# A network block on one core: front, first memory step and read-out in another order

## The reference

```
x = x + L0_conv(_ln_c(x))     # a memory: 16 steps over t, each one gradient step on a two-layer MLP per batch
t = t + L0_ffn(_ln_t(t))      # router, 8 experts, two chosen per token: gelu(xe @ W1 + b1) @ W2 + b2
x = x + L1_conv(_ln_c(x))     # small convolutions, applied over and over on channel groups
t = t + L1_ffn(_ln_t(t))      # a gated recurrence over 256 positions

def step(carry, x_t):                       # of L0_conv
    k = _l2norm(x_t @ Wk); v = x_t @ Wv
    lr, forget, eta = (means over c of sigmoid(x_t @ w_...))
    g = grad_fn(params, k, v)               # grad of mean((mlp(params, k) - v)**2)
    new_mom = eta * mom - lr * g;  new_params = params * (1 - forget) + new_mom
final = mean over b of paramsT;  return mlp(final, q)      # q = _l2norm(x @ Wq), the read-out
xe = xn * ln_g + ln_b                       # of L0_ffn, for each expert
```

## Time and profile before

| what | us |
|---|---|
| median of 3 runs (589.94 to 596.36) | 595.57 |
| the profiled execution, its own time | 592.88 |
| its span, first to last instruction | 591.1 |
| TensorE busy in the span | 537.3 |
| VectorE busy | 285.9 |
| ScalarE busy | 217.6 |
| GpSimd busy | 104.3 |

### The profile page before, as it was taken

How to read it: one execution, slowest core, us unless ns; L and a number is a source line. 1 busy time by engine, 2 the same in 40 slices (tenths; PEclk the granted TensorE clock), 3 DMA queues, 4 the chain that set the end, 5 groups by cost and what they waited for, 6 DMA issues and landing times.

```text
span 591.1 us, 10757 instructions
## 1 busy us (share of the span) xinstructions
PE 537.3 (91%) x3798; PEld 310.1 (52%) x3798; DVE 285.9 (48%) x1320; ACT 217.6 (37%) x1084; POOL 104.3 (18%) x103
## 2 busy tenths in 40 slices
PE   6799999999987999898799999999999999999996
PEld 4598888888744433377354444444444444444443
DVE  2636666666644744701734444444444444444443
ACT  1425555555423634010133333333333333333332
POOL 3227777777810000000000000000000000000000
PEclk9759999999988999999889999999999999999998
DMA  7400000000000000000000000000000000000000
GB/s 216 202 2 0 2 2 1 2 2 1 2 0 1 0 1 2 0 1 0 1 2 1 1 2 1 2 1 2 2 1 2 1 2 1 1 2 0 2 2 19
DMA packets 2871, 7.12 MB, mean 12 GB/s; under 512 B 1404, under 2 KB 1985, under 8 KB 2625
## 3 DMA queue, kind: packets, MB, share of 16 engines
q1 hardware_dynamic: 2818, 6.44, 3.1%
HBM read 6.18 MB, written 0.26 MB: 11 GB/s over the span
## 4 chain that ended last, share of the span: by engine, by line
PE 52%; DVE 24%; ACT 16%; issue 7%; POOL 1%; DVEq 0%; POOLq 0%
PE bk L652 14%; DVE bk L1143 8%; ACT gi L813 8%; DVE mem L1146 7%; ACT bk L817 6%; PE bk L538 4%; PE bk L609 4%; PE bk L556 2%; PE bk L463 2%; PE bk L422 2%; PE bk L444 2%; PE bk L432 2%; PE bk L362 1%; PE bk L355 1%; PE bk L394 1%
## 5 line engine op out<-in xcount | busy, mean ns | idle before, releaser
L668 PE MATMUL bk<-idle 128*64 128x512 bf16 x720 | 201.1, 385 | 0.0
L652 PEld LDWEIGHTS bk<-mem,lvh 65*64 65x64 f32 x1536 | 81.0, 138 | 145.4 <-DVE mem L1146 144.1
L652 PE MATMUL bk<-mem,lvh 65*64 65x4 f32 x1536 | 103.8, 207 | 23.4 <-DVE mem L1146 4.3
L813 ACT ACTIVATE gi<-bk 128x4 f32<-128x4 f32 x256 | 45.0, 176 | 151.6 <-PE bk L652 151.6
L1143 DVE TENSOR_TENSOR_SCAN bk<-gi 64x12 f32<-64x12 f32 x256 | 47.6, 186 | 107.0 <-ACT gi L813 107.0
L668 PEld LDWEIGHTS bk<-idle 128*64 128x64 bf16 x720 | 61.3, 112 | 22.9 <-issue 1.2
L1146 DVE SCALAR_TENSOR_TENSOR mem<-og,bk 64x4 f32<-64x4 f32 x256 | 38.4, 150 | 53.7 <-ACT bk L817 53.7
L817 ACT ACTIVATE bk<-bk 64x4 f32<-64x4 f32 x256 | 36.6, 143 | 40.8 <-DVE bk L1143 40.3
L1150 DVE SCALAR_TENSOR_TENSOR gi<-mem,bk 64x4 f32<-64x4 f32 x255 | 39.1, 153 | 8.8
L815 ACT ACTIVATE og<-bk 64x4 f32<-64x4 f32 x256 | 42.8, 167 | 0.1
L919 DVE TENSOR_TENSOR mem<-mem,bk 128x256 f32<-128x256 f32 x64 | 26.8, 421 | 18.1 <-PE bk L355 12.0
(11 more groups left out here) (266 smaller groups left out, 727.0 us busy)
## 6 DMA issues: line engine op xcount, KB each, us to landing
cw<-in_cw SPq DMA_DIRECT2D x1, 3456.0 KB, 11.2
w<-in_w SPq DMA_DIRECT2D x1, 520.0 KB
mem<-in_memw SPq DMA_DIRECT2D x1, 512.0 KB, 3.2
w<-in_w SPq DMA_DIRECT2D x1, 512.0 KB
xm<-in_xm SPq DMA_DIRECT2D x1, 256.0 KB, 2.6
xs<-in_x SPq DMA_DIRECT2D x1, 256.0 KB, 3.6
out<-xs SPq DMA_DIRECT2D x1, 256.0 KB, 2.0
consts<-in_consts SPq DMA_DIRECT2D x1, 134.0 KB, 2.5
```

The lines of the kernel that those rows point to most:

```text
L652: return nc.tensor.matmul(bk[row:row + D, 2 * (s // CH % 2) + k, c:c + B], lvh[:, g, :], hist[:, s, :], start=False, stop=True, skip_group ...
L668: nc.tensor.matmul(bk[0:D, 5, 0:FILL_N], idle[:, 0:D], idle[:, 128:128 + FILL_N], start=True, stop=True)
L813: nc.scalar.activation(gi[:, 2:2 + 3 * B:3], bk[:, bank, cols], ACT.Tanh).then_inc(sem("in_gate"), 1)
```

## The change

*POOL and SP.* `warm` is cleared first and has a semaphore of its own; `idle` and `xnT` have one each. `x2A` and `w1g` are cleared at the start too, and the product of expert weights and gain follows as soon as `w1` has landed, ahead of the first memory step. The loads of `c1p` and `c1last` move up in SP's list.

*Keys ahead of queries.* Squares, sums, roots, reciprocals and unit products are done in two halves, keys first.

*Moved on TensorE.* The three `c1p` products go to the front, two ahead of the key transposes and one behind. Gate spreading, Gram products and query transposes stand in the first step, between first and second layer; the Gram is made in eight products of up to 128 columns. ScalarE's copies of the queries and DVE's rates move along.

*Read-out.* `FS` is made in four parts, the first layer's part first, and TensorE waits for each part by itself. The bias row becomes sixteen products of one column each into `b1p` (one column for each half of an expert), which GELU adds as its bias. ScalarE takes `root(2)` ahead of the copy. The copies of the transposed tokens are shared out by halves, and two GELU groups stand ahead of the router's tanh.

The diff, with eight columns of indent taken away:

```diff
+b1p = sb("b1p", [128, E * HC])
...
+                        (c1p[:, :, :], "c1p", "ld_c1"), (c1last[:, :], "c1last", "ld_c1"),
...
-                        (c1p[:, :, :], "c1p", "ld_c1"), (c1last[:, :], "c1last", "ld_c1"),
...
-    nc.gpsimd.memset(idle[:, :], 0.0)
-    nc.gpsimd.memset(xnT[:, :], 0.0).then_inc(sem("idle"), 1)
+    nc.gpsimd.memset(warm[:, :], 0.0).then_inc(sem("warm"), 1)
+    nc.gpsimd.memset(idle[:, :], 0.0).then_inc(sem("idle"), 1)
+    nc.gpsimd.memset(xnT[:, :], 0.0).then_inc(sem("xnT_zero"), 1)
...
-    nc.gpsimd.memset(warm[:, :], 0.0).then_inc(sem("cleared"), 1)
+    nc.gpsimd.memset(x2A[:, :], 0.0)
+    nc.gpsimd.memset(w1g[:, :, :], 0.0).then_inc(sem("cleared"), 1)
+    pool.wait_ge(sem("cleared"), 1)
+    pool.wait_ge(sem("ld_w1"), 48)
+    nc.gpsimd.tensor_tensor(w1g[0:D, :, :], w1[0:D, :, :], wide(lng[:, :], H), ALU.mult).then_inc(sem("w1g"), 1)
...
-    nc.gpsimd.memset(w1g[:, :, :], 0.0)
-    nc.gpsimd.memset(x2A[:, :], 0.0).then_inc(sem("zeros"), 1)
-    pool.wait_ge(sem("zeros"), 1)
-    pool.wait_ge(sem("ld_w1"), 48)
-    nc.gpsimd.tensor_tensor(w1g[0:D, :, :], w1[0:D, :, :], wide(lng[:, :], H), ALU.mult).then_inc(sem("w1g"), 1)
...
+    pe.wait_ge(sem("ld_c1"), 32)
+    nc.tensor.matmul(bk[0:D + 1, 0, 0:D + 1], c1p[:, 2, :], c1last[:, :], start=True, stop=True).then_inc(sem("c1_ps"), 1)
+    pe.wait_ge(sem("c1"), 1)
+    nc.tensor.matmul(bk[0:D + 1, 1, 0:D + 1], c1p[:, 1, :], c1a[:, :], start=True, stop=True).then_inc(sem("c1_ps"), 1)
     pe.wait_ge(sem("KK"), 1)
+    pe.wait_ge(sem("c1"), 2)
     for n in range(NT):
...
-    pe.wait_ge(sem("ld_g"), 32)
-    pe.wait_ge(sem("glin"), 1)
-    for g in range(3):
-        ins = nc.tensor.matmul(bk[:, 2, g * B * T:(g + 1) * B * T], gsel[:, g, :], glin[:, :], start=True, stop=True)
-    ins.then_inc(sem("gate_ps"), 1)
-    pe.wait_ge(sem("QV"), 1)
-    for n in range(NT):
-        ins = nc.tensor.transpose(bk[:, 4 + n // 4, (n % 4) * 128:(n % 4 + 1) * 128], QV[:, n, :], ident)
-        if n % 4 == 3:
-            ins.then_inc(sem("qqT_ps"), 1)
+    pe.wait_ge(sem("gS"), 2)
+    nc.tensor.matmul(bk[0:D + 1, 2, 0:D + 1], c1p[:, 0, :], c1b[:, :], start=True, stop=True).then_inc(sem("c1_ps"), 1)
...
-            for k in range(1, T):
-                n = (k - 1) // 2
-                ins = nc.tensor.matmul(bk[:, 6 - k // 8, (k % 8) * TB:(k % 8 + 1) * TB], kblk[:, n * 128:(n + 1) * 128],
-                                       kblk[:, k * TB:(k + 1) * TB], start=True, stop=True)
-                if k % 8 == 7:
+            pe.wait_ge(sem("ld_g"), 32)
...
+            pe.wait_ge(sem("vneg"), 2)
+            for g in range(3):
+                ins = nc.tensor.matmul(bk[:, 7, 256 + g * B * T:256 + (g + 1) * B * T], gsel[:, g, :], glin[:, :],
+                                       start=True, stop=True)
+            ins.then_inc(sem("gate_ps"), 1)
+            for n in range(NT):
+                w = min(128, (T - 1 - 2 * n) * TB)
+                ins = nc.tensor.matmul(bk[:, 6 - n // 4, n % 4 * 128:n % 4 * 128 + w], kblk[:, n * 128:(n + 1) * 128],
+                                       kblk[:, (2 * n + 1) * TB:(2 * n + 1) * TB + w], start=True, stop=True)
+                if n % 4 == 3:
                     ins.then_inc(sem("gram_ps"), 1)
+            pe.wait_ge(sem("QV"), 1)
+            pe.wait_ge(sem("gS"), 2)
+            for n in range(NT):
+                ins = nc.tensor.transpose(bk[:, 3 + n // 4, (n % 4) * 128:(n % 4 + 1) * 128], QV[:, n, :], ident)
+                if n % 4 == 3:
+                    ins.then_inc(sem("qqT_ps"), 1)
...
+        else:
+            pe.wait_ge(sem("qq"), 2)
...
-    pe.wait_ge(sem("qq"), 2)
     pe.wait_ge(sem("FW"), 1)
...
+    pe.wait_ge(sem("FW"), 2)
...
+    pe.wait_ge(sem("FW"), 3)
...
+    pe.wait_ge(sem("FW"), 4)
...
-    pe.wait_ge(sem("ld_c1"), 32)
-    nc.tensor.matmul(bk[0:D + 1, 2, 0:D + 1], c1p[:, 2, :], c1last[:, :], start=True, stop=True).then_inc(sem("c1_ps"), 1)
     pe.wait_ge(sem("ld_w1"), 48)
-    for e in range(E):
-        ins = nc.tensor.matmul(bk[64:65, 4 + e // 2, (e % 2) * H:(e % 2 + 1) * H], lnb[:, e:e + 1], w1[:, e, :],
+    for k in range(E * HC):
+        ins = nc.tensor.matmul(bk[:, 4, k:k + 1], w1[:, k // HC, k % HC * 128:(k % HC + 1) * 128], lnb[:, k // HC:k // HC + 1],
                                start=True, stop=True)
-    ins.then_inc(sem("w1row_ps"), 1)
-    pe.wait_ge(sem("c1"), 1)
-    nc.tensor.matmul(bk[0:D + 1, 3, 0:D + 1], c1p[:, 1, :], c1a[:, :], start=True, stop=True).then_inc(sem("c1_ps"), 1)
-    pe.wait_ge(sem("c1"), 2)
-    nc.tensor.matmul(bk[0:D + 1, 2, 0:D + 1], c1p[:, 0, :], c1b[:, :], start=True, stop=True).then_inc(sem("c1_ps"), 1)
-    pe.wait_ge(sem("c1"), 3)
+    ins.then_inc(sem("b1_ps"), 1)
...
-    pe.wait_ge(sem("w1row"), 1)
+    pe.wait_ge(sem("w1g"), 1)
+    pe.wait_ge(sem("b1p"), 1)
...
-    act.wait_ge(sem("cleared"), 1)
+    act.wait_ge(sem("warm"), 1)
     table(ACT.Sqrt)
     root(1)
+    act.wait_ge(sem("xnT_zero"), 1)
...
-    nc.scalar.activation(qksq[:, :, :].rearrange("p (k n) c -> p k n c", n=4), qk, ACT.Square).then_inc(sem("qksq"), 1)
+    for a in (1, 0):
+        nc.scalar.activation(qksq[:, :, a * D:(a + 1) * D].rearrange("p (k n) c -> p k n c", n=4), qk[:, :, :, a * D:(a + 1) * D],
+                             ACT.Square).then_inc(sem("qksq"), 1)
     act.wait_ge(sem("qk_sq"), 1)
-    nc.scalar.activation(qkr[:, :, :], qkv2[:, :, :], ACT.Sqrt).then_inc(sem("qk_n"), 1)
+    nc.scalar.activation(qkr[:, 1, :], qkv2[:, 1, :], ACT.Sqrt).then_inc(sem("qk_n"), 1)
+    act.wait_ge(sem("c1_ps"), 1)
+    nc.scalar.copy(c1a[:, :], bk[0:D + 1, 0, 0:D + 1]).then_inc(sem("c1"), 1)
+    act.wait_ge(sem("qk_sq"), 2)
+    nc.scalar.activation(qkr[:, 0, :], qkv2[:, 0, :], ACT.Sqrt).then_inc(sem("qk_n"), 1)
+    act.wait_ge(sem("c1_ps"), 2)
+    nc.scalar.copy(c1b[:, :], bk[0:D + 1, 1, 0:D + 1]).then_inc(sem("c1"), 1)
...
-    for n in range(2):
-        act.wait_ge(sem("qqT_ps"), n + 1)
-        nc.scalar.copy(qq[:, :].rearrange("p (b t c) -> p t b c", b=B, t=T)[:, 8 * n:8 * n + 8, :, :],
-                       bk[:, 4 + n, :].rearrange("p (t b c) -> p t b c", t=8, b=B)).then_inc(sem("qq"), 1)
+    act.wait_ge(sem("c1_ps"), 3)
+    nc.scalar.copy(c1a[:, :], bk[0:D + 1, 2, 0:D + 1]).then_inc(sem("c1"), 1)
+    act.wait_ge(sem("cleared"), 1)
...
+        if t == 0:
+            for n in range(2):
+                act.wait_ge(sem("qqT_ps"), n + 1)
+                nc.scalar.copy(qq[:, :].rearrange("p (b t c) -> p t b c", b=B, t=T)[:, 8 * n:8 * n + 8, :, :],
+                               bk[:, 3 + n, :].rearrange("p (t b c) -> p t b c", t=8, b=B)).then_inc(sem("qq"), 1)
...
-    for k, dst in enumerate((c1a, c1b, c1a)):
-        act.wait_ge(sem("c1_ps"), k + 1)
-        nc.scalar.copy(dst[:, :], bk[0:D + 1, 2 + k % 2, 0:D + 1]).then_inc(sem("c1"), 1)
-        if k == 0:
-            act.wait_ge(sem("w1row_ps"), 1)
-            act.wait_ge(sem("w1g"), 1)
-            nc.scalar.copy(w1g[D:D + 1, :, :].rearrange("p (k n) h -> p k (n h)", k=4), bk[64:65, 4:8, :]).then_inc(sem("w1row"), 1)
     root(2)
+    act.wait_ge(sem("b1_ps"), 1)
+    nc.scalar.copy(b1p[:, :], bk[:, 4, 0:E * HC]).then_inc(sem("b1p"), 1)
...
-    for n in range(2):
-        act.wait_ge(sem("XT_ps"), n + 1)
-        nc.scalar.copy(x2A[0:D, n * 512:(n + 1) * 512], bk[0:D, 2 + n, :]).then_inc(sem("x2A"), 1)
+    act.wait_ge(sem("XT_ps"), 2)
+    nc.scalar.copy(t1T[64:128, 512:1024], bk[64:128, 3, :]).then_inc(sem("t1T"), 1)
+    nc.scalar.copy(x2A[0:D, 512:1024], bk[0:D, 3, :]).then_inc(sem("x2A"), 1)
...
-            nc.scalar.activation(hT[:, g % E, c, :], bk[:, 4 + (g * HC + c) % 4, :], ACT.Gelu).then_inc(sem("hT"), 1)
+            nc.scalar.activation(hT[:, g % E, c, :], bk[:, 4 + (g * HC + c) % 4, :], ACT.Gelu,
+                                 bias=b1p[:, g % E * HC + c:g % E * HC + c + 1]).then_inc(sem("hT"), 1)
+    for g in range(2):
+        gelus(g)
     act.wait_ge(sem("md"), 1)
     nc.scalar.activation(p1[:, :], md[:, :], ACT.Tanh, scale=0.5).then_inc(sem("p12"), 1)
-    for g in range(3):
-        gelus(g)
+    gelus(2)
...
-    dve.wait_ge(sem("qksq"), 1)
-    link(nc.vector.tensor_reduce(qkr[:, :, :], qksq[:, :, :].rearrange("p n (a c) -> p n a c", a=2), AX, ALU.add))
-    nc.vector.tensor_scalar(qkv2[:, :, :], qkr[:, :, :], 1e-24, None, ALU.max).then_inc(sem("qk_sq"), 1)
-    dve.wait_ge(sem("qk_n"), 1)
-    link(nc.vector.reciprocal(qkr[:, :, :], qkr[:, :, :]))
-    newton(qkr[:, :, :], qkv2[:, :, :], nt[:, :].rearrange("p (n a) -> p n a", a=2))
+    for k, a in enumerate((1, 0)):
+        dve.wait_ge(sem("qksq"), k + 1)
+        link(nc.vector.tensor_reduce(qkr[:, a, :], qksq[:, :, a * D:(a + 1) * D], AX, ALU.add))
+        nc.vector.tensor_scalar(qkv2[:, a, :], qkr[:, a, :], 1e-24, None, ALU.max).then_inc(sem("qk_sq"), 1)
...
-    unit(KK[:, :, 0:D], 1)
-    unit(KK[:, :, D:2 * D], 1).then_inc(sem("KK"), 1)
-    unit(QV[:, :, 0:D], 0)
```

(52 more changed lines are left out.)

22 lines of the change are left out of this document (11 added, 11 removed).

## The result

| what | before | after |
|---|---|---|
| median, first set (4 runs each) | 595.97 (589.94 to 597.24) | 577.17 (576.35 to 577.8) |
| the profiled execution | 592.88 | 577.29 |
| its span | 591.1 | 575.5 |
| mean granted clock in it | 0.963 | 0.974 |

The ratio is 0.9703 (95% interval 0.9636 to 0.977). The prediction said 579.5 and 574 to 587.

A forecast was written before the change was run, and what follows sets the result against it. Bound by TensorE without a break from 23.75 us in front, and by FS, L481, row copy and fillers in the read-out. Front 7.2 plus read-out 7.2 made 14.4 off 592.9, 578.5; against the middle of runs, 579.5 said; range 574 to 587.

The forecast's parts named there:

- Start, 0.8: Front: clearing the warm-up value first frees ScalarE's root from the other memsets; minus 0.8 of DVE's 0.85 us wait.
- Keys and masks: Front: keys-first halves make keys ready at 18.4; masks end and the first layer starts at about 22.0; conv-matrix products nothing.
- Reordering and Gram, 4.7: Front: second layer starts at 31.0 instead of 35.67, minus 4.7 us, with the Gram in sixteen passes taking 3.5.
- Clock, 3.0: Query transposes and first step: the 128-column Gram run brings full clock back; gain 3.0 us, bounds nothing to 4.3.
- w1g on POOL, 0.5: Front: POOL's 3.60 us product runs beside the keys' norms on DVE; plus 0.5 us, bounds 0 and 3.6.
- FS, 2.3: Read-out: POOL free and FS's first-layer quarter first, so L481 starts at the fillers' end, 162.27; minus 2.3 us.
- Level, 1.7: Read-out: without the gap the clock level holds, L481 takes 1.9 for 3.60; minus 1.7 us, bounds 0 and 1.7.
- part B: The read-out's share of the forecast: token transposes 7.0 us earlier plus 0.2 from token copies, 7.2 us in all.
- 1: First step: clock level stays down until the 256-column products at its end; part A loses 3.0, 582.5; chance 0.20.
- 3: Read-out: one-column products let the clock fall before fillers and first expert products; part B loses 3.5, 583.0; chance 0.13.
- Rival 2: Front: POOL's w1g product meets the keys' norms in full and holds DVE; part A loses 3.1, 582.6; chance 0.07.
- 4: Memory steps: front ends at half level and steps stay there, each 3.5 us more; slower, 603.5 with six; chance 0.03.

## Why the prediction was right, and where it was not

*What bounds the kernel.* Right: TensorE without a gap from the first layer to the second, and in the read-out the chain over FS, bias row and fillers.

*Start, 0.8.* Mis-sized: the reciprocal came at 6.36 for 6.75, so it gave 0.4, since DVE's addition ahead of the root took 0.75. "Root before 6 us" failed in after (6.12) and in two more kernels with the same order there (6.43 and 9.06), and held in three (5.51, 5.82, 5.82). Luck made up for it: the transposes of the normed input took 1.03 for 1.89, which brought the key products 0.7 forward and which no term of the sum held. In the four other kernels with the old order these transposes took 1.03 too, so it was the profile of before that had a slow draw.

*Keys and masks.* Keys ready at 18.08 (said 18.4), first layer at 22.50 (said 22.0). The conv-matrix products were taken at nothing if their copies end before the keys. They did not: the second copy ended at 19.62, since TensorE, whose gate products took 3.09 for 1.88 at half level, came to these products only at 18.46. DVE waited 1.05 for the queries' root behind the first copy, and the key transposes stood behind the second until 19.76. So both ways to the first layer ran through these products: DVE's masks ended at 22.45, and TensorE, behind ScalarE's table load and the gates' tanh, was free at 22.47. The term was mis-sized, by about 1 us in this execution (an estimate from DVE's wait; no run has the new order without these products in front). In the other kernels with the new order, leaving out the one with POOL's product during the norms, DVE's wait was 0 to 0.54.

*Reordering and Gram, 4.7.* The second layer started at 30.51 in the timeline (said 31.0), 5.2 earlier than before. What TensorE does between the gates and the second layer is one unbroken run, and it gained from the other order only what it starts earlier: 1.25 (22.50 for 23.75). The minus 5.1 that the working has for the first layer is mostly given back by gates and transposes, which now stand behind it. The rest is the Gram's shape, 2.85, and 1.1 of the query transposes (0.78 from the Gram's end to the second layer, for 1.90), which the clock gave. The experiments agree on the shape, which is worth 3.1 to the Gram and, with the clock, 3.5 to the step in the kernel that changes it alone. What the order is worth stays open. The run starts at 22.84 to 23.75 in the five profiles with the old order and at 20.86 to 22.59 in the seven with the new (again without the one where POOL's product was made to collide), 1.5 apart in the middle. The times say 2.3 with the 64-column Gram (586.02 and 583.68) and nothing with the 128-column one (581.92 and 583.61).

*The step behind the Gram.* "ScalarE's query copies lie beside the transposes but for the last" was too kind: TensorE waited for them until 31.40, 0.4 behind the end of the second layer's passes. The sum had no term for it.

*Clock, 3.0.* Right in kind, and too small: the first step took 38.45 - 30.51 = 7.94 for 11.13, which is 3.2, and with the 1.1 of the transposes the clock gave 4.3, the most that the working allowed. In cause the working was too sure: one kernel of nine with that run did not have the rise. Its example, L324, holds by the passes: in after the same products took 3.75 at a granted clock of 0.50, as L324's 3.70, and the level rose at 16.0, 2.3 behind their end. The Trainium skill (TensorE: Matmul & The Clock Gate, Part 4, PE-mode transpose) says that transposes don't count as busy for the clock; the trace does not decide it, since the level rose at 29.7 with the transposes just begun. No transposes followed the Gram in the kernel where it stayed down, nor in the one with the Gram's shape alone, where it rose at 30.6.

*w1g on POOL, 0.5.* Nothing in after: the product ended at 15.11, beside one sum of 0.69 that was not held. In the two kernels with POOL held back it ended at 15.22 and 15.38 and held a small operation of the norms for 0.2 and 0.6. Where they met in full the price was 2.2 to 3.0.

*FS, 2.3.* Right: four passes 1.88 behind the fillers' start for 4.19 (164.57 - 160.38). The cause, POOL, is shown by the held pair. The Trainium skill (SBUF — State Buffer, Who interferes with whom) says that VectorE's operations with two SBUF inputs contend with GpSimd's reads, and its scalar operations can contend in a two-port mode, the one that comes second waiting out the other. The held additions, 2.58 and 2.71, and the held scalar operation, 3.18, agree.

*Level, 1.7.* The number came out (1.72 for 3.60), the reason only in part. Behind the gap of 2.3 the four passes took 3.60, 3.20 and 1.96 in the three profiles that have it, 1.98 behind the gap of 1.20, and 1.88 in all nine without a gap. So the gap lets the level fall in some executions and not in others, and closing it is worth 0.1 to 1.7. The profile of before had the full price; with the 1.96 of the run with the root alone, part B would have given about 5.6 and not 7.3.

*Root, and what is late next.* Right: the root alone moved nothing, TensorE was next, with 3.52 for the bias products (said 3.9) and 4.73 for the fillers (said 4.79 or 3.3); 7.0 in all, as said. *Copies and GELU.* 0.3 for 0.2; GELU with the bias takes 0.69 for 0.60 (means of 32), and is covered.

*Rivals.* 1 did happen, in the kernel with read-out and Gram. 3 happened in a milder form: in the profiles with the one-column products and all fillers behind them the fillers took 4.4 to 4.9 for 3.3 (and in one of them, with POOL's block at the old place, the bias products 5.43 for 3.68). But before's fillers took that too (4.79), behind the bias row, so the one-column products are not shown to be the cause. In two kernels it was worse: bias products, fillers and first experts took 5.71, 6.13 and 6.93, and 5.95, 5.51 and 8.39. Rival 2 happened where it was forced. 4 did not: each step behind the first had its full clock.

*The distance between the two sets* fits the clock that each execution was granted; this is an estimate, from the mean clocks and the times. (The mean misses some of the time at half level: the rows of before show a granted clock of 1.00 from 5 to 21 us, yet its first transposes took 1.89 for the 1.03 of other executions.) In the first set it was 0.971 to 0.974, in the second 0.962 to 0.967. At half level TensorE spends 2 x (1 - clock) of the span: 29.9 us at 0.974 (2 x 0.026 x 575.5), 44.4 at 0.962 (2 x 0.038 x 583.9). The 14.5 between them cost up to half, 7.2, and the times are 8.4 apart (585.69 and 577.29). Before it is the same: 588.4 to 589.3 at 0.968 to 0.971, 590.3 to 591.2 at 0.962 to 0.963, 594.7 to 597.4 at 0.951 to 0.954. At like clocks (0.962 to 0.963) after (583.09 to 585.69) lies 5 to 8 below before. So of the 18.8 of the first set more than half is clock: partly the change's own, by the Gram, partly the draw of the set. Before's median was 595.97 over its 4 runs there and 590.4 to 591.2 in the three later sets of 11 to 13. Which stretches ran at half in the second set isn't shown, as none of its undisturbed executions was profiled.

## What to carry to other kernels

Where one engine works without a gap, moving its work about can gain no more than the gap at the front of the run; look for what makes the work itself shorter, as the Gram's wider products did here. Work that is put in front "for nothing" should be checked in every queue that it passes: the first of the two small copies for the convolutions held a root that DVE waited for. A term that rests on the granted clock should be priced from several executions, since the level that one profile shows in a stretch may be absent in the next. And a product or memset that is moved on POOL must be checked against every small DVE operation that it now runs beside, for an operation of 0.17 can last as long as POOL's does.

## What was not expected of the hardware

POOL's memsets held DVE's small addition ahead of the first root, for a length that differs from execution to execution: from 0.31, 0.40, 0.46, 0.75 and 1.05 to 3.69 us in the kernels with the new front. In the longest it waited past all the memsets in POOL's queue, to 9.03, and not only past the one it met. The change put two more memsets (0.95 and 1.80) into that queue and so made the longest hold possible. With POOL held back it took 0.17, in the two executions profiled; it took 0.17 beside the memsets too, in two profiles with the old front, so those two do not show that the hold is gone for good.

The clock's fall in the read-out was moved but not removed: fillers among the bias products put it behind the logits in one kernel and left it among the bias products in another.
